# Attention with a gated FFN on one core: V's product, its transpose and the gate's steps moved, tiles of scores grouped by shape, output products in pairs

## The reference

```
xn  = (x - mean) / sqrt(var + 1e-5)
q   = (xn Wq' + bq) / 4                       # 16 heads of 16
k,v = xn Wkv' + bkv                           # ONE head of 16 each
attn: softmax(q k') v for 16 heads, then Wo' and bo
ffn : gate = one-hot of argmax(xn w_gate)     # 6 experts, top 1
      a     = softmax(xn tokens_e' / 16)      # 100 tokens an expert
      delta = ((a[1:] val_e[1:]) + xn) wd' ...
      out   = log(sum_e exp(delta_e * scale) * gate_e), with a guard for 0
y   = x + attn + ffn
```

## Time and profile before

| | us |
|---|---|
| median of 3 runs | 894.55 (894.02 to 895.84) |
| the profiled execution | 893.1 |
| its span | 891.3 |
| tile 0 of batch 7 to tile 0 of batch 8 | 51.44 (394.23 to 445.67) |

### The profile page before, as it was taken

The page is one execution under the profiler, slowest core; times in us unless marked ns, Lnnn a source line. Parts: engine busy times, 40 slices in busy tenths (PEclk is TensorE's granted clock), DMA queues, the critical chain, the costliest instruction groups (busy, mean ns, idle before and its releaser), DMA issues.

```text
span 891.3 us, 18198 instructions
## 1 busy us (share of the span) xinstructions
PE 837.5 (94%) x6038; PEld 276.6 (31%) x6038; DVE 770.9 (86%) x1488; ACT 687.0 (77%) x1386; POOL 566.8 (64%) x754
## 2 busy tenths in 40 slices
PE   6679999999999999999999999999999999999987
PEld 4333223332323332332323233232333333232213
DVE  7688898989989898998989899898989899898926
ACT  2226888888888888888888878888887888888883
POOL 2874677676667767666677766667775766646321
PEclk7688999999999999999999999999999999999989
DMA  4413243634433443534444453443435345241112
GB/s 118 116 41 66 68 101 86 131 86 127 102 97 86 121 107 97 126 93 107 91 109 107 104 120 86 120 98 91 113 97 120 86 119 112 62 105 62 63 52 71
DMA packets 125076, 86.09 MB, mean 97 GB/s; under 512 B 57143, under 2 KB 109112, under 8 KB 124984
## 3 DMA queue, kind: packets, MB, share of 16 engines
q1 hardware_dynamic: 124504, 84.56, 38.5%
q10 hardware_dynamic: 480, 0.36, 0.1%
HBM read 39.30 MB, written 33.54 MB: 82 GB/s over the span
## 4 chain that ended last, share of the span: by engine, by line
PE 76%; DVE 14%; issue 4%; POOL 3%; ACT 2%; DMA 1%; DVEq 0%; POOLq 0%
PE pO L376 24%; PE pA L358 18%; PE pB L363 8%; DVE M L850 8%; PE pA L499 5%; PE pA L446 5%; PE pA L518 4%; PE pA L501 3%; PE pA L435 3%; PE pA L471 2%; PE pA L486 2%; ACT P L658 2%; DVE st L778 1%; PE pB L479 1%; DVE RL L863 1%
## 5 line engine op out<-in xcount | busy, mean ns | idle before, releaser
L850 DVE TENSOR_REDUCE M<-pA 128x1 f32<-128x512 f32 x1024 | 650.0, 681 | 80.3 <-PE pA L358 79.0
L658 ACT ACTIVATE P<-pB 128x512 f32<-128x512 f32 x1002 | 556.5, 605 | 124.8 <-PE pB L363 120.5
L358 PE MATMUL pA<-K,Q 48*128 48x512 f16 x1024 | 320.3, 388 | 27.0 <-DVE M L850 15.0
L363 PE MATMUL pB<-Q,K 50*128 50x512 f16 x1002 | 314.0, 385 | 0.3 <-DVE M L850 0.2
L376 PE MATMUL pO<-P,VK 128*32 128x512 f32 x2048 | 273.9, 607 | 2.0 <-ACT OTr L664 1.1
L358 PEld LDWEIGHTS pA<-K,Q 48*128 48x128 f16 x1024 | 67.8, 94 | 337.7 <-DVE M L850 273.7
L1005 POOL TENSOR_TENSOR Rs<-Rs,Cz 128x512 f32<-128x512 f32 x32 | 40.7, 1272 | 51.1 <-ACT Cz L646 49.0
L376 PEld LDWEIGHTS pO<-P,VK 128*32 128x32 f32 x2048 | 40.6, 108 | 96.7 <-issue 56.8
L998 POOL TENSOR_SCALAR Cz<-Cx 128x512 f32<-128x512 f32 x32 | 62.1, 1941 | 11.5 <-ACT Cx L640 11.5
L363 PEld LDWEIGHTS pB<-Q,K 50*128 50x128 f16 x1002 | 64.1, 94 | 7.4 <-ACT P L658 5.5
L963 POOL CAST Qp<-qf 128x512 f16<-128x512 f32 x31 | 18.9, 610 | 66.4 <-ACT qf L607 66.3
(11 more groups left out here) (170 smaller groups left out, 897.5 us busy)
## 6 DMA issues: line engine op xcount, KB each, us to landing
o_parts<-OTr SPq DMA_DIRECT2D x62, 256.0 KB, 2.2
X<-in_x SPq DMA_DIRECT2D x16, 512.0 KB, 3.9
q_pieces<-Qp SPq DMA_DIRECT2D x64, 128.0 KB
out<-OUT SPq DMA_DIRECT2D x32, 256.0 KB, 3.4
Op<-o_parts SPq DMA_DIRECT2D x31, 256.0 KB
Rb<-l_parts SPq DMA_DIRECT2D x31, 256.0 KB
Q<-q_pieces SPq DMA_DIRECT2D x30, 256.0 KB, 4.7
Q<-q_pieces SPq DMA_DIRECT2D x34, 128.0 KB, 4.6
```

Of the source, the lines that this page charges most:

```text
L358: e.matmul(bank1("ab", t)[:, :], Q16[r:r + 48, b % 3, h, 128 * s:128 * s + 128], K16[r:r + 48, b % 3, :], start=True, stop=True).then_inc( ...
L363: e.matmul(bankB(t)[:, :], K16[r:r + 50, b % 3, 128 * i:128 * i + 128], Q16[r:r + 50, b % 3, :, 32 * hh:32 * hh + 32], start=True, stop=Tr ...
L658: e.activation(P[:, u % PR, :], bankB(u + LB)[:, :], ACT.Exp, scale=alpha).then_inc(S("e"))
L850: e.tensor_reduce(M[:, t // 32 % 2, t % 2, t % 32 // 2:t % 32 // 2 + 1], bank1("ab", t)[:, :], AX, ALU.max, negate=True).then_inc(S("mx"))
```

## The change

It has five parts.

1. **Tiles in stretches of two and three.** A list `STRETCH` says at which tiles of a batch a stretch begins: 0, 2, 4, 7, 10, 12, 14, 16, 18, 21, 24, 26, 29, 32, 34, 36, 39, 42 and so on. The stretches at 4, 7, 18, 21, 26, 29, 36 and 39 have three tiles; there are 28 in a batch. PV 5 and PV 7 are moved from slot 4k + 1 to 4k + 0.5, since a stretch would span their slot.
2. **`vg`** goes from behind tiles 18 and 19 to directly behind PV 4, which stands ahead of tile 18, and into the ring of four. **`vt`** goes from behind tile 27 to directly behind the second q, ahead of tile 24; its copies `vte` from behind exp 27 to behind exp 25.
3. **The gate's five steps** get slots of their own: between maxima 27 and 31, one or two at a time, where they stood together behind maximum 28.
4. **The transposes `mt`** are made with a weight of 128 columns, half of them zeros, in place of 64, so that they have the shape of the d ahead of them; `d2` moves from behind tile 39 to behind tile 35, where it stands ahead of `mt`.
5. **The output products** stand in pairs: o0 and o1 behind tile 31, o2 and o3 behind tile 55. The second of each pair takes a bank of the ring of three.

A batch now reads: d 0 PV 2 d mt **4-6** PV **7-9** PV 10 q 12 PV 14 uk 16 PV vg **18-20** PV **21-23** q vt 24 PV **26-28** PV **29-31** o o 32 PV 34 d mt **36-38** PV **39-41** PV 42 s 44 PV 46 d 48 PV 50 p 52 PV 54 o o 56 PV 58 a 60 PV 62.

```diff
 SLOT = {
-    "kd": -41.6, "vg": -45, "vge": -44.3, ...
+    "kd": -41.6, "vg": -46.9, "vge": -46.3, ...
...
+STRETCH = (0, 2, 4, 7, 10, 12, 14, 16, 18, 21, 24, 26, 29, 32, 34, 36, 39, 42, 44, 46, 48, 50, 52, 54, 56, 58, 60, 62)
+PV_AT = {5: 0.5, 7: 0.5}
...
+    def stretch(n):
+        k = n % 64
+        first = max(m for m in STRETCH if m <= k) if n < NT else k - k % 4
+        return n - k + first + 0.02 * (k - first)
     for n in range(NT + LB):
-        put("ab", n - n % 2 + 0.02 * (n % 2) if n < NT else n - n % 4 + 0.02 * (n % 4), n)
+        put("ab", stretch(n), n)
...
     for v in range(NT // 4):
-        put("pv", 4 * (v + LV + (v + LV >= NT // 4)) + 1, v)
+        k = v + LV + (v + LV >= NT // 4)
+        put("pv", 4 * k + (PV_AT.get(k % 16, 1) if k < NT // 4 else 1), v)
...
-        M2 = sb("M2", [128, 2, 2, H], F16)
+        M2 = sb("M2", [128, 128], F16)
...
         FREED1 = {
-            "a": lambda b: (S("mm"), b + 1), ...
+            "a": lambda b: (S("mm"), b + 1), "vg": lambda b: (S("vge"), b + 1), ...
...
         FREED2 = {
-            "o3": lambda b: (S("fo"), 4 * b + 4),
+            "o1": lambda b: (S("fo"), 4 * b + 2), "o3": lambda b: (S("fo"), 4 * b + 4),
...
         def bankO(t, b):
-            return (bank2 if (t, b) == (3, NB - 1) else bank1)(f"o{t}", b)[:, 0:C]
+            return (bank2 if t == 3 or t == 1 and b < NB - 1 else bank1)(f"o{t}", b)[:, 0:C]
...
-                    e.transpose(bank2("mt", g)[:, :].bitcast(F16)[0:64, 0:128],
-                                M2[:, :, :, :].rearrange("p a k h -> p (a k h)"), idh[:, :]).then_inc(S("mt"))
+                    w.wait_ge(S("mz"), 1)
+                    e.transpose(bank2("mt", g)[:, :].bitcast(F16)[:, 0:128], M2[:, :], idh[:, :]).then_inc(S("mt"))
...
-                if (b := due("gate", n)) is not None:
+                if (b := due("gate0", n)) is not None:
                     w.wait_ge(S("gt"), b + 1)
                     e.tensor_reduce(gmx[:, :], G[:, :, :], AX, ALU.max).then_inc(S("g0"))
+
+                if (b := due("gate1", n)) is not None:
                     w.wait_ge(S("g0"), b + 1)
...
+            e.memset(M2[:, 64:128], 0.0).then_inc(S("mz"))
```

More of the change, by code:

```diff
@@ L52 @@
     "q0": -57, "qe0": -56, "qs0": -55, "qw0": -54, "uk": -53, "uke": -52, "ks": -51, "kd": -50, "q1": -52, "qe1": -51,
-    "qs1": -50, "vg": -50, "vge": -50.5, "vt": -48, "vte": -47, "gate": -46, "mask": -45, "qw1": -40, "mkd": -39,
+    "qs1": -50, "vg": -50, "vge": -50.5, "vt": -48, "vte": -47, "gate0": -46, "gate1": -45.9, "gate2": -45.8, "gate3": -45.7, "gate4": -45.6, "mask": -45, "qw1": -40, "mkd": -39,
     "utm": -30, "s": 9, "smax": 9.6, "sexp": 10.2, "ssum": 10.8, "snorm": 11.4, "p": 17, "pte": 17.6, "a": 21, "mm": 21.6,
@@ L64 @@
 }
-LAST_BUT_ONE = {"o3": 171, "fo3": 171.6, "st1": 172.2}
+LAST_BUT_ONE = {"o2": 167, "fo2": 167.6, "o3": 171, "fo3": 171.6, "st1": 172.2}
 TAIL = {
@@ L89 @@
 DVE_NAMES = ("rngq", "rng", "two", "scl", "wl", "scd", "stats0", "stats1", "stats2", "stats3", "aggr", "refine", "xl0", "xl1",
-             "qs0", "gate", "smax", "ssum", "mm", "mx", "rec", "fo0", "fo1", "fo2",
+             "qs0", "gate0", "gate1", "gate2", "gate3", "gate4", "smax", "ssum", "mm", "mx", "rec", "fo0", "fo1", "fo2",
              "fo3", "nl00", "nl01", "nl02", "nl03", "nl10", "nl11", "nl12", "nl13")
@@ L265, in build @@
         ld = nc.dram_tensor("l_parts", (4, 8 * T), F32, kind="Internal").ap()
+        M2v = M2[:, 0:64].rearrange("p (a k h) -> p a k h", a=2, k=2)
         def bc(ap, n):
@@ L283, in build @@
             "uk": lambda b: (S("uke"), b + 1), "q0": lambda b: (S("qe0"), b + 1), "q1": lambda b: (S("qe1"), b + 1),
-            "a": lambda b: (S("mm"), b + 1), "rg": lambda b: (S("two"), 2), "bs": lambda b: (S("scl"), 1),
+            "a": lambda b: (S("mm"), b + 1), "vg": lambda b: (S("vge"), b + 1), "rg": lambda b: (S("two"), 2), "bs": lambda b: (S("scl"), 1),
             "o0": lambda b: (S("fo"), 4 * b + 1), "o1": lambda b: (S("fo"), 4 * b + 2),
-            "o2": lambda b: (S("fo"), 4 * b + 3), "o3": lambda b: (S("fo"), 4 * b + 4),
+            "o2": lambda b: (S("fo"), 4 * b + 3),
             "d0": lambda b: (S("cx"), 4 * b + 1), "d1": lambda b: (S("cx"), 4 * b + 2),
@@ L296, in build, with turns @@
             "sl0": lambda b: (S("rl"), 4),
-            "o3": lambda b: (S("fo"), 4 * b + 4),
+            "o1": lambda b: (S("fo"), 4 * b + 2), "o3": lambda b: (S("fo"), 4 * b + 4),
         }
-        def turns(freed, first, last, o3):
+        def turns(freed, first, last, o1):
             return sorted((n, name, key) for name in freed for n, key in at[name].items()
                           if (name != "ab" or first <= key < last and key not in at["bd"].values())
-                          and (name != "o3" or key in o3))
-        TURNS = (turns(FREED1, 0, NT, range(NB - 1)), turns(FREED2, LB, NT + LB, (NB - 1,)))
+                          and (name != "o1" or key in o1))
+        TURNS = (turns(FREED1, 0, NT, (NB - 1,)), turns(FREED2, LB, NT + LB, range(NB - 1)))
         TURN = tuple({(name, key): k for k, (_, name, key) in enumerate(t)} for t in TURNS)
@@ L512, in _ @@
                         parts = 2 if b < NB - 1 else 1
-                        w.wait_ge(*(before2 if (t, b) == (3, NB - 1) else before1)(f"o{t}", b))
+                        w.wait_ge(*(before2 if t == 3 or t == 1 and b < NB - 1 else before1)(f"o{t}", b))
                         w.wait_ge(S("onl"), 2 * b + parts)
@@ L817, in _ @@
                                     ALU.mult).then_inc(S("g2"))
+                if (b := due("gate3", n)) is not None:
                     w.wait_ge(S("g2"), b + 1)
                     e.tensor_reduce(gm2[:, :], gw[:, :, :], AX, ALU.max).then_inc(S("g3"))
+                if (b := due("gate4", n)) is not None:
                     w.wait_ge(S("g3"), b + 1)
```

18 lines of the change are left out of this document (9 added, 9 removed), and 8 rows, old and new, of the table SLOT.

## The result

The changed kernel takes 931.1 us (929.76 to 931.68, 4 runs) against 894.28 (893.19 to 895.84, 4 runs): ratio 1.041, 95% interval 1.039 to 1.043. It is slower, as forecast, but by 36.8 us where 27.5 were forecast, and the time lies above the range (909 to 928). The profiled execution has a span of 928.0 against 891.3.

The account below looks back on a forecast made before the run. TensorE sets the pace; per batch 4.87 us of added waits less 2.04 of removed waits and 0.95 on shapes gives +1.88. Fourteen batches (26.3) plus 1.2 for batch 15 give +27.5, so 922 us, range 909 to 928.

Parts of the forecast that it names:

- the middle batch: One of the repeating batches: 53.3 us instead of 51.44, net +1.88.
- The saving on shapes: TensorE, fewer changes of matmul shape: 0.9 to 1.0 us saved a batch, taken as 0.95.
- PV 5 behind tile 18: PV 5 waits for exp 19 behind tiles 18 to 20: 1.60 against 0.76, 0.84 us, plus vg's reading and tile 20.
- PV 7 behind tile 26: PV 7 waits for exp 27 behind tiles 26 to 28: starts 1.60 after the stretch against 0.76, 0.84 us.
- tile 26 behind tile 24: Tile 26's B waits for vt's bank: starts 2.54 after tile 24 where 1.54 is needed, 1.01 us.
- PV 2 behind tile 7: PV 2 waits for exp 7 behind tiles 7 to 9: 1.11 against 0.76, 0.34 us.
- tile 6 behind tile 4: Tile 6 waits for the copy of mt, which takes a turn in the ring of three: 0.33 us, 0.8 behind tile 4.
- tile 33's wait: Tile 33's B waits for tile 31's bank, as o1 has a turn of the ring: 3.13 against 2.41, 0.72 us.
- the clock falls in the longer waits: Rival: one 1.5 us piece a batch at 1.2 GHz takes twice as long, +1.5 a batch, 944 us; chance 0.03.
- Batch 0 and the tail: 0: First batch and the end of the kernel: the change adds nothing there; batch 15 was put separately at about +1.2 us.
- the rings answer in time: Rival: copies and exp 31 come before TensorE asks, only PV and mt wait: +0.15 a batch, 896.8 us; chance 0.05.
- shapes are what counts: Rival, faster: exponentials ready at each PV, -0.59 a batch, 886 us; no bank waits either, 851 us; chance 0.06.

Follow-up runs that it names:

- b_stretch: Kernel before with vg, vt in the ring of four, 128-column mt, gate steps apart, plus the change's stretches, PV 5/7 slots, o0 and d2 moved: 905.51 us.
- fill: Changed kernel plus 16 zero-weight matmuls a batch, eight behind PV 6 and eight ahead of PV 7: 924.06 us.
- tail_o3: Changed kernel with only the o3 of batch 14, in the tail, in the ring of four: 926.44 us.
- b_mt: Kernel before with only the transposes mt made with a weight of 128 columns, half zeros: 893.03 us, ratio 0.998.
- o_four: Changed kernel with o1 and o3 of all batches but the last back in the ring of four, pairs kept: 917.84 us.
- copies_early: Changed kernel with vt's two copies on ScalarE behind exp 24, ahead of the reading of q, instead of behind exp 25: 915.44 us.
- early_ofour: Changed kernel with vt's copies ahead of the reading of q, and o1 and o3 in the ring of four: 907.24 us.
- vg_hide: Changed kernel with vg moved to between tile 20 and PV 5, its reading on ScalarE behind exp 20: 920.05 us.

## Why the prediction was right and where it failed

**What held.** The sign, and the middle batch: 53.25 against 53.3. The saving on shapes: TensorE's busy time fell by 1.09 a batch, I had 0.95. The waits by place, with the start that was forecast and the one measured: PV 5 behind tile 18 1.7, 1.72; PV 7 behind tile 26 1.60, 1.58; tile 26 behind tile 24 2.54, 2.54; PV 2 behind tile 7 1.11, 1.10 (tile 7 at 5.46 and tile 10 at 7.56 of the batch, less PV's 1.00); tile 6 behind tile 4 0.78, 0.81. Only tile 33's wait was too large, 0.72 for a measured 0.59 (0.82 less 0.23); ScalarE's second small step came 0.73 behind exp 29 and not 0.86. The experiments confirm that these are the causes and not only neighbours: the edits at tile 26, tile 33 and PV 5 each shortened the batch there, and b_stretch shows the stretches of three alone at 1.56 a batch. PV 2, PV 10 and the two mt were not taken away one by one; for them the start times speak, and b_stretch for all together.

**What failed, first: the clock was dismissed.** The step that failed is the rival that the clock falls in the longer waits, with a chance of 0.03, against which I put a window of batch 15 with TensorE busy 6.54 of 8.00 and the full clock. That window's waits are some 0.5 us; the change has waits of 0.84, 0.94 and 0.75 within 9 us, and behind them the clock fell, in 5 of 13 like batches, for 5.5 us in all. `fill` shows the cause. The price that I gave it, 1.5 us a batch in every batch, was too high, and the conclusion that it needn't be in the sum wrong.

**Second: the tail.** "Batch 0 and the tail: 0" is the other term. I had seen that o1 and o3 take turns in the ring of three and worked that out for the middle batch alone. In the tail the same turn falls behind the bank of the row sums, which is held until the fourth of VectorE's reciprocals. `tail_o3` puts 3.35 us to it. Batch 15 and the tail together are 4.15 where I had 1.2.

**Third, small and open:** up to tile 0 of batch 1 it is 1.80 more where I had 0. The clock rises there at 77.3 us in the one profile and at 74.4 in the other, and over the experiments batch 0 takes 55.6 to 59.8, so I can't give it to the change. Batches 1 to 14 at the full clock came to 25.25 of the 26.3 forecast.

So the mechanisms of a middle batch were right, and with the two missed terms, 5.5 and some 3, the forecast would have been 930.5. That this comes within 1 us of the measured time is in part luck: the 1.80 of batch 0 and the 1.05 that batches 1 to 14 came in below the sum go opposite ways. The range was too narrow for what it left out: it was built from the errors of the terms that I had, not from a term that I had not.

The rivals: that the rings answer in time did not happen (tile 26 waited its full 1.0). That shapes are what counts did not either; a change of shape does cost some 0.1 us (in b_mt 0.11 at tile 4), but all ten of the change together, 1.09 of TensorE's busy time, are worth hardly more than the one wait of 1.0 us at tile 26. Two prices of rivals were out by 1 to 2 us: by 14 batches 851 would be 853 and 944 would be 943; nothing rests on them.

## What to carry to other kernels

Before two products are moved together to save a change of shape, ask what stood between them: here each of the small products between the tiles was also the time in which ScalarE answered. The quickest test is to read two numbers in a stage with nothing else in the way, from the start of a product to the start of what reads its result and from a bank's release to its next use, and to hold the new order against them. A step that is given a turn in another ring must be followed through every place where that turn falls, the tail too, and where a change adds long waits to TensorE in a row, a price for the clock belongs into the sum.

## What the runs showed of the hardware that I had not expected

- The granted clock fell from 2.4 to 1.2 GHz for 3.4 us in the middle of a stream in which TensorE is busy 49.17 of 53.25 us, behind three waits of 0.75 to 0.94; it made the products there up to twice as long, 1.10 a time. The same batch does it in some repetitions and not in others: in the profiled executions 5 of 13 in the changed kernel and in `tail_o3`, 1 in `o_four` (52.90 a batch), none in `copies_early` (52.53), `early_ofour` (52.20) and `vg_hide` (52.88).
- 16 matmuls of zeros a batch in the waits prevented all of these and cost nothing to be seen: 53.23 a batch with them, 53.25 without. Work that produces nothing made the kernel 7 us faster.
- The profile's clock row and the length of one like product (0.23 or 0.41 from tile to tile) tell the same story; the busy time of TensorE alone would have hidden it, since it rises in such a batch (50.38 us for 49.17).
